# GpSimd waits for a batch's gathers to land before it issues the next batch's

## The chip, the cores and the metric

The kernel runs on one core of a Trainium2 chip. The core has TensorE (PE, matrix products), VectorE (DVE), ScalarE (ACT), GpSimd (POOL), SyncE (SP, which only issues transfers) and 16 DMA engines that all queues share. The metric is the device time of one execution in microseconds (us), lower is better.

## What is computed

Two layers, each of the form x + s * silu(g), on x of 8 batches of 512 tokens with 256 channels. The second layer, in whose last part the change lies:

```python
xn = _layernorm(x)
s = _hyena_fwd(xn, ...)      # projection, short convolution, long convolution by FFT, gate, projection
# g: a mixture of 20 experts, the 2 best of each token
top_vals, top_idx = jax.lax.top_k(probs, K)                     # K = 2
y = sum over e of gates[:, e] * (xf @ We[e] + be[e])            # gates: 0 but for the two chosen experts
x = x + s * _silu(y)
```

The first layer is causal attention with 16 heads (s) and a gated feed-forward network (g). All inputs and the output are float32.

## The kernel before

The kernel has three stages. Every engine runs its own program for each stage, and semaphores order them against each other.

**Attention stage.** It makes the first layer for each batch, normalises its result, picks two experts a token and scatters the token's row into `slots_in`, a table sorted by expert, with eight indirect transfers of 128 rows a batch (line 664, issued by GpSimd).

**Experts' stage.** 84 blocks of 128 rows are loaded from `slots_in`, multiplied with their expert's matrix (line 2032), get their expert's bias (line 2090) and go to `slots_out` (line 2062). It ends some 842 us into the span.

**Convolution stage.** It runs over the batches b = 0 to 7. A turn of TensorE is `pe_turn(b)`: the projection of batch b+1 (line 340), the first inverse product of b (line 373), the transposes of b+1 (line 362), the second inverse product of b (line 373), the forward transform of b+1 (line 317, four parts of 12 matmuls, each part with one increment of `vf_ps` at its end) and the output projection of b (line 408). ScalarE copies the projection out of PSUM (`projected`, line 419), does the first tap of the short filter (line 428), splits v into its high part (line 434), scales the rows of the first expert of a token (`first_choice`, line 2130), copies the four parts of the spectrum out of PSUM (`transformed`, line 442) and takes the silu (line 2136). VectorE multiplies the spectrum with the filter (`with_filter`, lines 481 to 524), does the other taps (line 457), the low part of v (line 464), the gate (line 551), adds the rows of the second expert (`second_choice`, line 2142), adds the output bias (line 558) and finishes the result (lines 2150 and 2154). Each engine takes these steps in the order written in `convolution_scalar`, `convolution_vector` and `pe_turn`.

GpSimd's only work in this stage is to gather the experts' rows of each token from `slots_out`: for batch n eight indirect transfers of 128 rows (two experts, four tiles of tokens) into `yg[:, n % 2]`, each adding 16 to `got[n % 2]`, so that a batch adds 128. `yg` has two buffers. Batch n's gathers may start when `acc_sb` is at n - 1, that is when VectorE has added the second expert's rows of batch n - 2 and the buffer is free. `acc_sb` at or below zero is not waited for, so batches 0 and 1 have no such wait. Ahead of each batch's gathers stands a one-column multiply into `idle_q` (line 2251), in a chain with itself over the semaphore `idle`. The users of the rows, `first_choice` and `second_choice`, wait for `got` themselves.

Of the kernel before, what the change touches and what calls it, by code (L numbers as in the profile page):

```python
# [47 lines left out]
def at_least(eng, sem, value):  # L48

    if isinstance(value, int) and value <= 0:  # L50
        return
    eng.wait_ge(sem, value)

def program(nc, x, wqkvT, woutT, wguT, wdT, wg1, bg1, wg2, bg2, winT, bin_, short, wo2, bo2, fw1, fb1, fw2, fb2,
# [15 lines left out]
    with ctx:  # L71
# [2042 lines left out]
        X = {n: sem("x_" + n) for n in "idle prem acc_sb sg_sb prod out_sb".split()}  # L2114
# [127 lines left out]
        def convolution_gpsimd(pool):  # L2242
            pool.wait_ge(W["kept"], NBLK)
            pool.memset(vt[:, :, 0:1], 0.0)
            pool.memset(vt[:, :, T + 1:T + 2], 0.0).then_inc(U["edges"], 1)
            for h_ in range(2):
                pool.wait_ge(yb_out[h_], 16 * NI)
            for n in range(B):
                at_least(pool, X["acc_sb"], n - 1)
                at_least(pool, X["idle"], n)  # L2250
                pool.tensor_tensor(idle_q[:, 3:4], ramp_col[:, :], ramp_col[:, :], ALU.mult
                                   ).then_inc(X["idle"], 1)
                for k in range(TOPK):
                    for t in range(NT):
                        pool.indirect_dma_start(yg[:, n % 2, k, t, :], None, slots_out,  # L2255
                                                bass.IndirectOffsetOnAxis(pos[:, n, t, k:k + 1], axis=0)
                                                ).then_inc(X["got"][n % 2], 16)

        with nc.Block() as block:
            @block.sync  # L2260
            def _(sp):
                attention_sync(sp)
                experts_sync(sp)
                convolution_sync(sp)

            @block.tensor
            def _(pe):
                attention_tensor(pe)
                experts_tensor(pe)
                convolution_tensor(pe)  # L2270

            @block.scalar
            def _(act):
                attention_scalar(act)
                experts_scalar(act)
                convolution_scalar(act)

            @block.vector
            def _(dve):
                attention_vector(dve)  # L2280
                experts_vector(dve)
                convolution_vector(dve)

            @block.gpsimd
            def _(pool):
                attention_gpsimd(pool)
                convolution_gpsimd(pool)
# [57 lines left out]
```

## Time and profile before

| | us |
|---|---|
| median of 3 runs | 1039.91 (1037.98 to 1041.28) |
| profiled execution | 1047.65 |
| its span, first to last instruction | 1045.9 |
| TensorE busy in the span | 954.6 (91%) |
| VectorE busy | 685.5 (66%) |
| ScalarE busy | 467.8 (45%) |
| GpSimd busy | 327.5 (31%) |

Times in rows are us from the span's start. A row of the timeline has the start, the duration, the engine, the source line, the operation, output and inputs, the form and the count of merged instructions; in brackets stands the engine's idle time before it and what ended it ("issue": nothing that the profile shows; "remote": a semaphore that moved long after the instruction that should have moved it). TensorE's rows show when a matmul is issued; its end is modelled, so that when its result was there is seen from those who wait for it. Shares of busy time are averages over the whole span; the change concerns its last 200 us alone.

### The profile page before, as it was taken

How to read it: one execution, taken by the hardware profiler on the slowest of the kernel's cores; microseconds unless marked ns; L12 is line 12 of the kernel's file. 1: busy time of each engine (PE TensorE's matmuls, PEld its weight loads, DVE VectorE, ACT ScalarE, POOL GpSimd, SP SyncE). 2: the span in 40 equal slices, each digit the busy share in tenths (PEclk: the TensorE clock that was granted, in tenths of full speed). 3: DMA queues.
4: the chain of work that ended last, by engine and by line, in shares of the span. 5: the costliest groups of instructions: out<-in, count | busy, mean ns of one | idle time of the engine just before them, and what ended most of it. 6: DMA issues, size and time to landing. Idle time of an engine off the chain costs nothing.

```text
span 1045.9 us, 18938 instructions
## 1 busy us (share of the span) xinstructions
PE 954.6 (91%) x5844; PEld 720.9 (69%) x5844; DVE 685.5 (66%) x1451; ACT 467.8 (45%) x871; POOL 327.5 (31%) x605
## 2 busy tenths in 40 slices
PE   8789999999999999999999999775889995999996
PEld 6666865866776775775776766464657783888885
DVE  6474676667577577577577466444566334899998
ACT  4346456446455555545546545442222332444442
POOL 5223224513612613613614522513000044322220
PEclk9899999979999999999999997986999996999999
DMA  7955856335535534644544620456876652443431
GB/s 268 117 152 88 184 139 88 110 131 79 113 141 83 122 141 71 124 151 63 102 161 63 134 82 2 142 157 197 250 235 209 193 181 67 125 156 123 132 106 44
DMA packets 88187, 136.70 MB, mean 131 GB/s; under 512 B 9987, under 2 KB 63939, under 8 KB 86084
## 3 DMA queue, kind: packets, MB, share of 16 engines
q1 hardware_dynamic: 69636, 100.75, 40.0%
q0 software_dynamic: 6144, 16.79, 5.3%
q10 hardware_dynamic: 12352, 18.48, 5.1%
q8 instruction: 28, 0.46, 0.2%
q14 instruction: 27, 0.22, 0.1%
HBM read 79.36 MB, written 55.57 MB: 129 GB/s over the span
## 4 chain that ended last, share of the span: by engine, by line
PE 32%; issue 31%; POOL 13%; DVE 11%; SPq 4%; ACT 2%; DMA 2%; another core or an unknown queue 1%; POOLq 0%; DVEq 0%; ACTq 0%
POOL PT L1850 6%; PE PS L2032 5%; PE PS L1053 3%; PE PS L373 3%; PE PS L1067 3%; PE PS L1025 3%; POOL slots_in L664 3%; PE PS L317 3%; DVE tmp L481 3%; POOL h L1833 3%; PE PS L828 3%; SPq L1968 2%; PE PS L340 2%; POOL idle_p L1844 2%; SPq L1972 1%
## 5 line engine op out<-in xcount | busy, mean ns | idle before, releaser
L1562 DVE TENSOR_REDUCE Mneg<-PS 128x2 f32<-128x1024 f32 (+2 forms) x192 | 195.0, 1043 | 70.3 <-PE PS L1029 69.3
L1316 ACT ACTIVATE PT<-PS 128x512 f32<-128x512 f32 (+1 forms) x384 | 172.7, 530 | 122.8 <-PE PS L1053 120.8
L1025 PE MATMUL PS<-ks,qs 96*128 96x256 f32 (+3 forms) x512 | 122.0, 348 | 3.1 <-issue 2.1
L1053 PE MATMUL PS<-qs,ks 96*128 96x512 f32 (+3 forms) x512 | 122.2, 358 | 2.6 <-ACT PT L1316 1.5
L1844 POOL TENSOR_TENSOR idle_p<-neghalf 128x1 f32<-128x1 f32 x128 | 25.2, 196 | 307.7 <-ACT PT L1316 307.7
L1053 PEld LDWEIGHTS PS<-qs,ks 96*128 96x128 f32 x512 | 89.1, 195 | 37.5 <-ACT PT L1316 18.4
L828 PE MATMUL PS<-xnT,Wgu 128*128 128x512 f32 x384 | 103.3, 410 | 8.5 <-DVE h L1505 8.4
L2032 PE MATMUL PS<-Wes,xbT 128*128 x336 | 98.6, 405 | 3.4 <-issue 2.5
L1850 POOL TENSOR_SCALAR_AFFINE_SELECT PT<-PT 128x256 f32<-128x256 f32 x256 | 98.9, 410 | 0.0
L1067 PE MATMUL PS<-PT,V 128*32 128x512 f32 (+3 forms) x1024 | 88.0, 451 | 5.9 <-POOL PT L1850 4.9
L828 PEld LDWEIGHTS PS<-xnT,Wgu 128*128 128x128 f32 x384 | 69.9, 191 | 31.4 <-DVE h L1505 11.8
L1025 PEld LDWEIGHTS PS<-ks,qs 96*128 96x128 f32 x512 | 77.7, 197 | 14.0 <-issue 10.0
L2090 DVE TENSOR_TENSOR yb<-PS,bes 128x256 f32<-128x256 f32 x84 | 35.3, 424 | 59.0 <-PE PS L2032 47.7
L2032 PEld LDWEIGHTS PS<-Wes,xbT 128*128 128x128 f32 x336 | 54.5, 197 | 22.6 <-issue 19.4
L1833 POOL TENSOR_TENSOR h<-h,h 128x512 fp32r<-128x512 f32 x40 | 51.3, 1290 | 59.4 <-ACT h L1280 59.2
L2054 ACT ACTIVATE xbT<-PS 128x256 f32<-128x256 f32 x84 | 31.5, 383 | 84.4 <-PE PS L2015 73.6
L664 POOL DMA_INDIRECT slots_in<-xn,rows_now x64 | 62.4, 975 | 17.5 <-issue 17.2
L2255 POOL DMA_INDIRECT yg<-slots_out,pos x64 | 61.5, 961 | 18.6 <-issue 17.6
L1505 DVE SCALAR_TENSOR_TENSOR h<-PS,sil 128x512 f32<-128x512 f32 x48 | 32.5, 689 | 49.4 <-ACT sil L1273 38.3
L1029 PE MATMUL PS<-mask,ident 128*128 128x128 f16 (+2 forms) x352 | 63.8, 257 | 0.0
L317 PE MATMUL PS<-v,Fwd 128*128 128x256 f32 x432 | 56.8, 291 | 6.0 <-issue 6.0
L373 PE MATMUL PS<-Inv,Z 128*128 128x256 f32 x256 | 58.5, 382 | 3.0 <-DVE Z L522 2.5
(239 smaller groups left out, 1604.3 us busy)
## 6 DMA issues: line engine op xcount, KB each, us to landing
qs<-qk_parts SPq DMA_DIRECT2D x96, 128.0 KB
ks<-qk_parts SPq DMA_DIRECT2D x96, 128.0 KB
slots_out<-yb ACTq DMA_DIRECT2D x28, 384.0 KB, 3.3
xb<-slots_in SPq DMA_DIRECT2D x83, 128.0 KB, 2.8
qk_parts<-qhl SPq DMA_DIRECT2D x16, 512.0 KB, 2.7
qk_parts<-khl SPq DMA_DIRECT2D x16, 512.0 KB, 3.1
xn2T_parts<-xn2T SPq DMA_DIRECT2D x8, 1024.0 KB, 4.9
xT<-xn2T_parts ACTq DMA_DIRECT2D x7, 1024.0 KB
```

The lines of the kernel that those rows point to most:

```text
L317: last = pe.matmul(PS[:, bank, C * (q_ % 2):C * (q_ % 2) + C], Fwd[:, i, kc, P * q_:P * q_ + P], src[:, j, 2 * half + kc, :], start=n == 0 ...
L373: last = pe.matmul(PS[:, 6 + m, C * z:C * z + C], Z[:, z, c, P * m:P * m + P], Inv[:, c, :], start=c == 0, stop=c == NQ - 1)
L664: pool.indirect_dma_start(slots_in, bass.IndirectOffsetOnAxis(rows_now[:, t, k:k + 1], axis=0), xn2[:, t, :], None).then_inc(S["sent"], 16)
L828: last = pe.matmul(out, lhs(i, c), rhs(j, c), start=last is None, stop=n == 0)
L1025: pe.matmul(out, qs[:, hd, P * qt:P * qt + P], ks[:, hd, 0:keys], start=n % a_bank == 0, stop=False, skip_group_check=True)
L1053: last = pe.matmul(PS[:, 4 + n, col:col + T - P * kt], ks[:, hd, P * kt:P * kt + P], qs[:, hd, P * kt:T], start=True, stop=True)
L1067: last = pe.matmul(PS[32 * j:32 * j + 32, 7, P * kt:T], V[:, kt, GH * g + j, :], PT[:, g % 2, j, COL[kt]:COL[kt] + T - P * kt], start=kt = ...
L1316: act.activation(PT[:, g % 2, j, 512 * n:512 * n + width], PS[:, 4 + n, 0:width], ACT.Exp, scale=SCALE).then_inc(S["exped"], 1)
L1562: dve.tensor_reduce(out=Mneg[:, 0, qt, heads[0]:heads[-1] + 1], in_=all_of, op=ALU.max, axis=AX.X, negate=True).then_inc(S["maxed"], 1)
L1833: pool.tensor_tensor(h[:, i, LO, :], h32[:, i % 2, :], f(h[:, i, HI, :]), ALU.subtract).then_inc(S["h_lo"], 1)
L1850: last = pool.affine_select(out=blocks, in_=blocks, compare_op=ALU.is_ge, fill=0.0, base=0, pattern=[[0, 2], [1, P]], channel_multiplier=-1)
L2032: ins = pe.matmul(PS[:, HALF + u % HALF, 0:C], xbT[:, u, c, :], Wes[:, bass.ds(expert, 1), c, :].rearrange("p o n -> p (o n)"), start=c == ...
```

## The change

After the wait for `acc_sb` and ahead of the multiply, GpSimd also waits, from batch 1 on, until `got` of the batch before is complete, that is until all eight of its gathers have landed.

```diff
             for n in range(B):
                 at_least(pool, X["acc_sb"], n - 1)
+                if n > 0:
+                    pool.wait_ge(X["got"][(n - 1) % 2], 128 * ((n - 1) // 2 + 1))
                 at_least(pool, X["idle"], n)
                 pool.tensor_tensor(idle_q[:, 3:4], ramp_col[:, :], ramp_col[:, :], ALU.mult
                                    ).then_inc(X["idle"], 1)
```

## Rows read from the trace of the kernel before

**Rows 1.** Timeline of VectorE: second expert's rows, filter products, split of v.

```profile
861.48 1.67 DVE L2142 SCALAR_TENSOR_TENSOR acc<-yg,gates,acc 128x256 f32<-128x256 f32 x4 [4.35 <-ACT acc L2130]
...
902.11 0.69 DVE L481 TENSOR_TENSOR tmp<-Vf,HA 128x512 f32<-128x512 f32 x1 [1.23 <-ACT Vf L442]
...
925.75 0.69 DVE L481 TENSOR_TENSOR tmp<-Vf,HA 128x512 f32<-128x512 f32 x1 [1.09 <-ACT Vf L442]
...
944.35 1.22 DVE L464 TENSOR_TENSOR v<-PS,v 128x1024 fp32r<-128x1024 f32 x1
...
949.43 0.69 DVE L481 TENSOR_TENSOR tmp<-Vf,HA 128x512 f32<-128x512 f32 x1 [1.09 <-ACT Vf L442]
```

**Rows 2.** Timeline of GpSimd: gathers and the multiply ahead of a batch.

```profile
847.73 1.32 POOL L2255 DMA_INDIRECT yg<-slots_out,pos  x1 [0.51 <-issue]
...
856.88 0.94 POOL L2255 DMA_INDIRECT yg<-slots_out,pos  x1 [0.30 <-issue]
...
858.19 0.98 POOL L2255 DMA_INDIRECT yg<-slots_out,pos  x1 [0.15 <-POOL idle_q L2251]
...
877.35 0.95 POOL L2255 DMA_INDIRECT yg<-slots_out,pos  x1 [0.30 <-issue]
900.96 0.19 POOL L2251 TENSOR_TENSOR idle_q<-ident 128x1 f32<-128x1 f32 x1 [22.67 <-DVE acc L2142]
...
957.54 0.95 POOL L2255 DMA_INDIRECT yg<-slots_out,pos  x1 [0.30 <-issue]
```

**Rows 3.** Timeline of TensorE: first turn, and a later one.

```profile
842.89 5.74 PE L340 MATMUL PS<-xT,Win 128*128 128x512 f32 x24 [0.69 <-DVE yb L2090]
...
856.05 5.74 PE L317 MATMUL PS<-v,Fwd 128*128 128x256 f32 x45
862.68 0.28 PE L317 MATMUL PS<-v,Fwd 128*128 128x256 f32 x1 [0.88 <-issue]
...
882.96 7.83 PE L340 MATMUL PS<-xT,Win 128*128 128x512 f32 x24
...
945.62 6.02 PE L317 MATMUL PS<-v,Fwd 128*128 128x256 f32 x48
...
954.74 5.83 PE L340 MATMUL PS<-xT,Win 128*128 128x512 f32 x24
```

**Rows 4.** Two windows: length, busy time of PE, PEld, DVE, ACT, POOL; clock, DMA share, GB/s.

```profile
862.00:867.00 5.00, 1.19 (x5) 0.79 (x5) 1.15 (x3) 0.00 (x0) 4.02 (x4) 0.99 0.38 105
867.00:872.00 5.00, 3.43 (x7) 1.57 (x6) 0.92 (x2) 0.60 (x1) 3.99 (x5) 0.50 0.35 102
```

**Rows 5.** Timeline of ScalarE: first expert's rows, spectrum copies, split of v.

```profile
859.74 1.71 ACT L2130 ACTIVATE acc<-yg,gates 128x256 f32<-128x256 f32 x4 [5.73 <-DMA yg<-slots_out,pos]
...
870.45 0.60 ACT L442 ACTIVATE Vf<-PS 128x512 f32<-128x512 f32 x1 [8.53 <-remote]
881.73 1.08 ACT L442 ACTIVATE Vf<-PS 128x512 f32<-128x512 f32 x2 [10.68 <-remote]
...
942.02 1.02 ACT L434 ACTIVATE v<-PS 128x1024 fp32r<-128x1024 f32 x1 [2.23 <-PE PS L362]
```

**Rows 6.** DMA queues from 862 to 882 (packets, MB, share): the answer's only queue.

```profile
q0 software_dynamic: 672, 1.84, 32.3%
```

**Rows 7.** Timeline of ScalarE: copies of the projection, first turn and a later one.

```profile
844.72 0.69 ACT L419 ACTIVATE vt<-PS,binc 128x512 f32<-128x512 f32 x1 [4.77 <-PE PS L340]
...
958.73 0.69 ACT L419 ACTIVATE vt<-PS,binc 128x512 f32<-128x512 f32 x1 [5.51 <-PE PS L340]
960.19 0.69 ACT L419 ACTIVATE vt<-PS,binc 128x512 f32<-128x512 f32 x1 [0.77 <-PE PS L340]
```

**Rows 8.** Timeline of all engines at the last burst of scatters.

```profile
719.93 0.57 PE L1238 MATMUL PS<-spread,ones 128*128 128x84 f32 x4
720.60 0.96 POOL L664 DMA_INDIRECT slots_in<-xn,rows_now  x1 [0.30 <-issue]
...
723.15 0.24 DVE L1780 TENSOR_SCALAR block_expert<-PS 128x84 int32<-128x84 f32 x1 [3.94 <-remote]
```

## The prediction

> **What bounds the kernel now.** I first asked what the changed line can touch: the stage in which all five engines run the convolution and mix the experts' rows, from 842 us of the span to its end. I read that stage engine by engine in the timeline. From the third turn on it is VectorE's: the first filter product of a batch starts at 925.75 and the next one's at 949.43 [rows 1], so a turn takes 23.68 us, and between these two VectorE sits idle for little but the 1.09 us ahead of each. GpSimd is far from that bound: the eight gathers of a batch, from 847.73 to 857.82 for batch 0, take 10 us [rows 2]. A later gather would therefore cost nothing in itself.
>
> The first turn does not look like that. The filter products of batch 1 could start when VectorE has added the second expert of batch 0, at 861.48 + 1.67 = 863.15; those of batch 2 start only at 902.11 [rows 1]. That is 38.96 us, where the later turns take 23.68. The missing 15.3 us lie in TensorE's rows: 45 of the 48 transform matmuls (line 317) of batch 1 go out at full pace, then single matmuls with 0.9 to 1.5 us between them, put down to "issue", until at 882.96 the next projection starts [rows 3]. From the transform's start to the next projection this turn takes 882.96 - 856.05 = 26.91 us, a later one 954.74 - 945.62 = 9.12 [rows 3]. In the same stretch the granted clock falls to 0.50, the lower level of 1.2 GHz, after TensorE has already been mostly idle for 5 us at 0.99 [rows 4], so the clock follows the stall and is not its start.
>
> ScalarE's rows tell what kind of stall it is. Its second spectrum copy starts at 870.45 after 8.53 us of idle time with the releaser "remote", the next at 881.73 after 10.68 us [rows 5]. Each waits only for matmuls that TensorE's own rows have as issued before 861.8 [rows 3]. So matmuls go in and their completions come out late, and in the end come all at once. Inside a part of the transform no matmul waits for a semaphore, and the only DMA queue with packets between 862 and 882 is GpSimd's, q0, at 32% of the engines [rows 6]: neither the experts' weights nor code are being loaded.
>
> What runs beside it is GpSimd. It issues 24 gathers without a break, 847.73 to 878.30 [rows 2]: batch 1 and batch 2 have both buffers and no acc_sb that is still missing. From batch 3 on it waits for acc_sb and issues eight at a time (for batch 3 until 900.96, after 22.67 us of idle time) [rows 2]. Two more places bear on whether a gather burst and late completions belong together. In a later turn ScalarE's first projection copy starts at 958.73, 3.99 us after the projection's first matmul, and the second at 960.19; the burst's last issue ends at 958.49 [rows 2, 3, 7]. With the first projection of the stage, before any gather runs, it is 844.72 - 842.89 = 1.83 us [rows 3, 7]. And at 719.93 four matmuls for the block table end a burst of scatters whose last issue ends at 721.56; VectorE gets their result only at 723.15, "remote" [rows 8]. So late in a burst of eight the completions are 2 to 3 us late, they come free 0.2 to 1.7 us after the burst, and after 24 in a row it takes until 881.73, 3.4 us. I read this as something that fills during a run of software gathers and empties when the run ends. What it is, the trace does not say.
>
> **The change, part by part.** It adds seven waits to GpSimd, one ahead of each batch from 1 on; it removes and moves nothing else. Behind the waiting instruction stand only the small multiply and this batch's eight gathers; the queues of SP and of ScalarE are not passed.
>
> Batches 3 to 7: the landing that is asked for is long past. Batch 3 asks for batch 2, issued by 878.30, at 900.96 [rows 2]; the later ones wait for acc_sb a turn further on in the same way. Cost 0, and the cover is the wait for acc_sb; without it a batch would start its gathers 1.9 us later, still ten microseconds or so before they are used.
>
> Batch 1: the last gather of batch 0 ends its issue at 857.82, and ScalarE gets the rows at 859.74 [rows 2, 5]. So the pause is 1.9 us and batch 1's gathers run from 860.1 to 870.1 instead of 858.19 to 868.2. Batch 2: one more such pause, 872.4 to 882.4, landed by 884.3. As data neither is missed: batch 1 is used 6.5 us ahead of VectorE's next filter product (in a later turn right behind the split of v, at 942.02 + 1.02 = 943.0 against 949.43 [rows 1, 5]), which is 880.4 even if that turn comes 15 us earlier, 8 us after the landing at 872.0.
>
> What the pauses do to the stall is the sum. If they empty what had filled, TensorE finishes the transform by 862 and the output projection by 865.2 (9.12 us after 856.05), ScalarE copies the spectra behind its mixing from 861.4 on, and VectorE starts batch 1 at 863.2 and batch 2 at 863.2 + 23.68 = 886.9 instead of 902.11: 15.2 us gained, with VectorE next in line. What is late next: the third burst now lies at 9 to 19 us of VectorE's turn, and its late part (from some 7 us into it, 879.5, to 1.7 us after it, 884.1) meets the transposes and the second inverse product, on which ScalarE's split of v at 942.02 - 925.75 = 16.3 us and VectorE's at 18.6 us of the turn wait [rows 1, 5]. Bounds: nothing, if VectorE's own work covers it; or VectorE's split, due at 881.8, waits for a release at 884.1 and ScalarE's 1.02 us: 3.3 us. I take the middle, 1.7, since the late completions of the later turns fall on cover and tell no more. Sum: -15.2 + 1.7 = -13.5 us, between -15.2 and -11.9. The profiled execution would go from 1047.65 us (span 1045.9 and 1.75 around it) to 1034.1, and the median of the runs from 1039.91 to 1026.4.
>
> The profiled execution is 7.74 us above that median, so the stall might not be in the plain runs. If it were in the profile alone, the plain runs should come, other things equal, to 1047.65 - 15.2 = 1032.4 or less; they are 7.5 us longer. That speaks for a stall in both.
>
> The Trainium skill, "Runtime: NRT & Kernel Launch", section "The ~15µs preamble/postamble breakdown", says that a profile's total is some 6.2 us above the reported execution time, whatever the kernel. By it 1047.65 would stand for 1041.4, which is close to the median and leaves the stall in the plain runs; no run here shows that figure by itself.
>
> **The rivals.** First, the stall belongs to the recording. For it: TensorE holds back matmuls that no semaphore is tied to, and VectorE and ScalarE, with few instructions, show no late completion of their own. Against it: the 7.5 us above. Then the plain runs have no such stall, the pauses cost and give nothing, and the time stays at 1039.9. 
> Second, slower: the pause is too short. If what fills needs longer than 1.9 us to empty, as the 3.4 us after 24 gathers could mean, it is not empty when batch 1's gathers begin, the stall goes on through batches 1 and 2 and ends as now 3.4 us after the last gather, which comes 3.8 to 4.1 us later: 1043.9. It decides at 1.9 us; the later bursts of eight come free in 0.2 to 1.7 [rows 2, 7], on the near side of it. 0.12.
>
> Third, the change does not reach the stall: it comes from something in the first turn other than the run's length, such as ScalarE's late start on the spectra behind the first gathers, at 859.74. The time stays at 1039.9. The late completions at other bursts speak against it. 0.06.
>
> **How the numbers follow.** The forecast, 1026.4, gets 0.57, since three bursts show the same lateness and the short ones come free by themselves. Its own range is 1023 to 1029: the bounds 1024.7 and 1028.0, and the runs' own spread of up to 1.9 us below and 1.4 above the median. The whole range goes on to 1041.5, to take in the two cases without an effect (0.31, at 1038.0 to 1041.3), and leaves out the slower one and the tails: about 0.2. A measurement of this kernel tells some 0.3% (3.1 us) from no change. Faster by more than that 0.57, within it 0.31, slower 0.12.
>
> **What would show it.** In the profile after: GpSimd idle for 1.9 us ahead of batches 1 and 2; no "remote" wait of the spectrum copies; transform and output projection of batch 1 done by 866; granted clock 1.00 from 862 to 890; VectorE's products of batch 2 at 887 to 890. If all of that is there and the plain time stays, the stall was the recording's. If single matmuls with a microsecond between them still stand from 862 to 885, the pause was too short or the reason is another; the forecast is wrong in both cases.

## The result and the profile after

| | before | after |
|---|---|---|
| median of the runs, us | 1040.60 (1037.98 to 1052.73, 4 runs) | 1063.34 (1061.53 to 1070.96, 4 runs) |
| profiled execution, us | 1047.65 | 1061.53 |
| its span, us | 1045.9 | 1059.8 |
| convolution stage in it: first projection matmul to the span's end, us | 1045.9 - 842.89 = 203.0 | 1059.8 - 833.71 = 226.1 |
| GpSimd busy, us | 327.5 | 418.5 |

The kernel became slower: 1.0219 times the time before, 95% interval 1.0181 to 1.0258, some 22.7 us. The forecast was 13.5 us faster, and the result lies above the whole range. Where the stage begins differs from execution to execution, with the same code in front of it (833 here, 843 before), so what follows compares the stage's own length: 23.1 us more, about what the medians say. Medians here and below are of all runs; the ratios leave out a run more than 1.5% above the fastest of its kernel, which of the changed kernels concerns one run, in the experiment of the cheap gap.

The stall that the prediction is about is gone. Timeline of TensorE after, first turn (columns as ahead of the rows of before):

```profile
846.92 6.10 PE L317 MATMUL PS<-v,Fwd 128*128 128x256 f32 x48
852.86 3.61 PE L408 MATMUL PS<-Wo,o 128*128 128x256 f32 x16
856.12 5.83 PE L340 MATMUL PS<-xT,Win 128*128 128x512 f32 x24
```

All 48 transform matmuls run as one group and the next projection starts 9.20 us after the transform's first matmul, against 26.91 before [rows 3] and 9.12 in the forecast. ScalarE, after, confirms it: its four spectrum copies run as one group, with no "remote" between them [rows 5].

```profile
850.58 1.71 ACT L2130 ACTIVATE acc<-yg,gates 128x256 f32<-128x256 f32 x4 [5.70 <-DMA yg<-slots_out,pos]
852.19 2.03 ACT L442 ACTIVATE Vf<-PS 128x512 f32<-128x512 f32 x4
```

What is new stands on GpSimd. Its timeline after: batch 1, the held gather of batch 2, the start of batch 3 and one gather of batch 7.

```profile
850.62 0.20 POOL L2253 TENSOR_TENSOR idle_q<-ident 128x1 f32<-128x1 f32 x1 [1.91 <-DMA yg<-slots_out,pos]
850.96 0.99 POOL L2257 DMA_INDIRECT yg<-slots_out,pos  x1
...
853.50 0.95 POOL L2257 DMA_INDIRECT yg<-slots_out,pos  x1 [0.30 <-issue]
854.75 9.09 POOL L2257 DMA_INDIRECT yg<-slots_out,pos  x1 [0.30 <-issue]
864.15 2.69 POOL L2257 DMA_INDIRECT yg<-slots_out,pos  x1 [0.30 <-issue]
867.15 1.02 POOL L2257 DMA_INDIRECT yg<-slots_out,pos  x1 [0.30 <-issue]
868.48 3.36 POOL L2257 DMA_INDIRECT yg<-slots_out,pos  x1 [0.30 <-issue]
872.14 0.95 POOL L2257 DMA_INDIRECT yg<-slots_out,pos  x1 [0.30 <-issue]
877.06 0.20 POOL L2253 TENSOR_TENSOR idle_q<-ident 128x1 f32<-128x1 f32 x1 [3.97 <-issue]
...
880.31 9.91 POOL L2257 DMA_INDIRECT yg<-slots_out,pos  x1 [0.31 <-issue]
...
905.80 0.19 POOL L2253 TENSOR_TENSOR idle_q<-ident 128x1 f32<-128x1 f32 x1 [5.07 <-issue]
...
1022.20 12.92 POOL L2257 DMA_INDIRECT yg<-slots_out,pos  x1 [0.31 <-issue]
```

The pause of 1.91 us is there as forecast. But from the fourth gather of batch 1 on, one gather in each burst takes 9.1 to 12.9 us to issue, and in batches 1 to 6 two more take 2.7 and 3.4, where those of before took 0.94 to 1.32 [rows 2]. The burst of batch 1 takes 872.14 + 0.95 - 850.96 = 22.1 us instead of 10, the later ones 22 to 23. Two lines of the view by source line say it for all 64 (durations in ns: smallest, median, largest); the first is after, the second before.

```profile
L2257 POOL DMA_INDIRECT yg<-slots_out,pos x64: 943/996/12922, 838.4 to 1040.4; - x64
```

```profile
L2255 POOL DMA_INDIRECT yg<-slots_out,pos x64: 940/946/1324, 847.7 to 1004.9; - x64
```

VectorE's timeline after tells when such a gather comes free:

```profile
853.91 0.69 DVE L481 TENSOR_TENSOR tmp<-Vf,HA 128x512 f32<-128x512 f32 x1
...
862.94 1.28 DVE L558 TENSOR_TENSOR s<-PS,bo2b 128x512 f32<-128x512 f32 x2
...
865.94 2.73 DVE L457 SCALAR_TENSOR_TENSOR cv<-vt,shortc,cv 128x512 f32<-128x512 f32 x4
...
869.79 1.22 DVE L2150 TENSOR_TENSOR acc<-sg,s 128x1024 f32<-128x1024 f32 x1
871.05 1.23 DVE L2154 TENSOR_TENSOR sg<-acc,x1b 128x1024 f32<-128x1024 f32 x1
...
878.70 1.67 DVE L2142 SCALAR_TENSOR_TENSOR acc<-yg,gates,acc 128x256 f32<-128x256 f32 x4 [2.81 <-ACT acc L2130]
880.29 0.68 DVE L481 TENSOR_TENSOR tmp<-Vf,HA 128x512 f32<-128x512 f32 x1
...
889.33 1.28 DVE L558 TENSOR_TENSOR s<-PS,bo2b 128x512 f32<-128x512 f32 x2
...
1022.18 0.68 DVE L481 TENSOR_TENSOR tmp<-Vf,HA 128x512 f32<-128x512 f32 x1
...
1034.22 0.68 DVE L558 TENSOR_TENSOR s<-PS,bo2b 128x512 f32<-128x512 f32 x1
```

Take 0.95 us, the undisturbed issue, off the end of a held gather: 854.75 + 9.09 - 0.95 = 862.89, 880.31 + 9.91 - 0.95 = 889.27, 1022.20 + 12.92 - 0.95 = 1034.17. Each time that is 0.05 to 0.06 us before VectorE starts line 558, the first instruction behind fifteen filter products (in the last turn twenty) that takes an input from PSUM. The 2.69 us gather gives 864.15 + 2.69 - 0.95 = 865.89, where line 457, a scalar_tensor_tensor, starts at 865.94. The 3.36 us gather gives 868.48 + 3.36 - 0.95 = 870.89. There no input comes from PSUM, but VectorE has a gap: line 2154 waits for line 2150 and starts 1.26 us behind it, where the next instruction of the same size, line 464 at 872.19, starts 1.14 us behind line 2154. So a gather, once it is held, stays held for as long as VectorE goes from one tensor_tensor with both inputs in SBUF straight to the next.

Not every such row holds a gather. In the kernel before, products follow each other 0.60 to 0.65 us apart, and the gathers beside them take 0.95 us; in the burst that begins at 948.75 all but the first start within 0.01 us of a product, as the gather of 957.54 [rows 2] does:

```profile
957.54 0.72 DVE L481 TENSOR_TENSOR tmp<-Vf,HN 128x512 f32<-128x512 f32 x1
```

From the first held gather on the engines run in lock step. The waits of the stage after (us in total, times, longest):

```profile
ACT acc L2130 <- DMA yg<-slots_out,pos: 68.9, 8, 19.7
...
DVE acc L2142 <- ACT acc L2130: 42.6, 8, 10.0
POOL idle_q L2253 <- issue: 27.5, 6, 5.1
```

Before, the first two were 5.7 and 4.3 us, once each, for batch 0, and GpSimd's third was a wait for `acc_sb`. Now ScalarE waits for rows in each turn, and behind that wait stand the four spectrum copies of the next batch. GpSimd's own wait ("issue" in the row) ends with the landing of the burst, within 0.1 us of ScalarE's start on its rows (876.96 and 877.06 for the rows of batch 1). It takes 4.0 to 5.1 us (for batch 2, 5.07 us; between 899 and 906 queue q1 moves 1.05 MB beside it), and only then do the next eight start. A turn is now GpSimd's: 905.80 - 877.06 = 28.74 us, of which 5.07 are the landing and 23.67 the burst. VectorE's first products of batches 2 and 7 are at 880.29 and 1022.18: 28.38 us a turn, where before it was 23.68 [rows 1]. The chain that ended last in after runs through the same gathers:

```profile
1014.48 4.47 issue
1018.95 0.20 POOL idle_q L2253
...
1022.20 12.92 POOL yg L2257
...
1040.44 2.72 DMA yg<-slots_out,pos
...
1043.18 0.03 ACT acc L2130
```

The account of the stage: up to the products of batch 2, 880.29 - 833.71 = 46.58 us against 902.11 - 842.89 = 59.22, so 12.64 gained; five turns of 4.70 us more, 23.5 lost; from the products of batch 7 to the end 37.6 against 1045.9 - 1020.49 = 25.4, 12.2 lost, since the last burst's rows arrive at 1043.18. Sum: +23.1 us.

### The profile page after: what moved, and what is told of

It is laid out like the page before. It is cut to its first block and busy times, and to the rows that moved or that the text cites. A ratio compares the mean times of both kernels' runs of the same rounds, so it can differ in the third digit from the quotient of the medians.

```text
span 1059.8 us, 18939 instructions
## 1 busy us (share of the span) xinstructions
PE 953.1 (90%) x5844; PEld 722.8 (68%) x5844; DVE 685.2 (65%) x1451; ACT 466.3 (44%) x871; POOL 418.5 (39%) x605
## 5 line engine op out<-in xcount | busy, mean ns | idle before, releaser
L2257 POOL DMA_INDIRECT yg<-slots_out,pos x64 | 151.5, 2367 | 21.2 <-issue 21.1
L1844 POOL TENSOR_TENSOR idle_p<-neghalf 128x1 f32<-128x1 f32 x128 | 25.4, 198 | 302.1 <-ACT PT L1316 302.1
L1025 PE MATMUL PS<-ks,qs 96*128 96x256 f32 (+3 forms) x512 | 118.8, 341 | 3.2 <-issue 2.1
L1053 PE MATMUL PS<-qs,ks 96*128 96x512 f32 (+3 forms) x512 | 118.4, 349 | 2.6 <-ACT PT L1316 1.5
L1053 PEld LDWEIGHTS PS<-qs,ks 96*128 96x128 f32 x512 | 85.6, 188 | 36.7 <-ACT PT L1316 19.1
L1025 PEld LDWEIGHTS PS<-ks,qs 96*128 96x128 f32 x512 | 75.5, 192 | 14.6 <-issue 8.9
L373 PE MATMUL PS<-Inv,Z 128*128 128x256 f32 x256 | 65.9, 416 | 5.8 <-DVE Z L522 4.1
L373 PEld LDWEIGHTS PS<-Inv,Z 128*128 128x128 f32 x256 | 53.6, 213 | 15.9 <-DVE Z L522 4.5
```

The lines of the kernel that those rows point to most:

```text
L373: last = pe.matmul(PS[:, 6 + m, C * z:C * z + C], Z[:, z, c, P * m:P * m + P], Inv[:, c, :], start=c == 0, stop=c == NQ - 1)
L1025: pe.matmul(out, qs[:, hd, P * qt:P * qt + P], ks[:, hd, 0:keys], start=n % a_bank == 0, stop=False, skip_group_check=True)
L1053: last = pe.matmul(PS[:, 4 + n, col:col + T - P * kt], ks[:, hd, P * kt:P * kt + P], qs[:, hd, P * kt:T], start=True, stop=True)
```

## The experiments

Each ratio below stands beside runs of the kernel before on the same chip; the chips differ (medians of before 1041 to 1050 us). Theory A: a gather is held while VectorE's filter products run without a gap, if the run itself began straight behind another instruction. In the kernel before each run of products starts out of 1.1 us of idle time [rows 1] and the gathers get in at instruction boundaries; in after, VectorE goes from the second expert's addition straight into the products, because that addition is what comes last. The loss then comes from the held gathers together with the lock step. Theory B: the form of the new wait makes the gathers slow. Theory C: a burst that begins inside a run of products is shut out, wherever the run started from.

**A wait ahead of the products (after plus one line).**

```diff
                 if b > 0:
+                    dve.wait_ge(X["sg_sb"], b)
                     for part in range(FILTER_PARTS - 2):
```

> The changed kernel with one more wait: VectorE waits for ScalarE's silu of the batch before (sg_sb) ahead of the filter products of batches 1 to 7, so that the run of filter products starts after 1 to 2 us of idle time instead of right behind the second expert's rows. Theory A (a run that starts behind another VectorE instruction shuts the gathers out; one that starts out of idle time lets them in): the gathers of batches 1 to 7 go back to 0.95 us each, a burst to 10 us, a turn from 28.4 to 24 to 26 us, and the time to 1030 to 1045. Theory B (the separate wait instruction of GpSimd does it) and theory C (what decides is that the burst reaches into a run that has begun): the third gather of a burst still takes some 9 to 10 us, and the time stays at 1061 to 1075.

1070.81 us, 1.0158 times before (1.0083 to 1.0233). The gathers are back at about 0.95 (mean 1.02 us over all 64, from 2.37), and GpSimd waits for `acc_sb` again, but the wait has a price of its own. Waits of the stage:

```profile
POOL idle_q L2254 <- DVE acc L2142: 80.9, 5, 19.4
...
DVE tmp L481 <- ACT sg L2136: 30.3, 6, 5.1
```

The silu is finished 5.05 us after VectorE would have begun, in each of six turns. A turn takes 28.95 us (batches 2 to 7), not the 24 to 26 expected. So the part of theory A on the gathers holds; the expected time failed, since the silu comes so much later than the edit assumed. A cheaper gap is needed (below).

**The form of the wait (before plus one line).**

```diff
                 at_least(pool, X["acc_sb"], n - 1)
+                if n > 1:
+                    pool.wait_ge(X["got"][n % 2], 128 * ((n - 2) // 2 + 1))
```

> The kernel before with a wait of the same form at the same place, but for the landing of batch n - 2, which is long past when GpSimd comes to it (from batch 2 on). Theory B (form of the wait): a gather of 9 us in each burst, and 1055 us or more. Theories A and C: gathers of 0.95 us, single matmuls a microsecond apart in the first turn as before, 1036 to 1050 us, no change from the kernel before.

1049.60 us against 1050.10, 0.9992 (0.9961 to 1.0022). The wait asks for the landing of the batch before last, which is long past.

```profile
L2257 POOL DMA_INDIRECT yg<-slots_out,pos x64: 942/948/1167, 840.1 to 1002.2; - x64
```

No gather is above 1.17 us. Here the wait never blocks; in the experiment ahead the change's own waits stand and the gathers are quick as well. So theory B falls.

**The third burst and all later ones held into the products (before plus one line).** `dstep` counts VectorE's filter products; the line makes GpSimd wait for the third of a turn, for batches 2 to 7.

```diff
                 at_least(pool, X["acc_sb"], n - 1)
+                if n > 1:
+                    pool.wait_ge(U["dstep"], ND * (n - 1) + 3)
```

> The kernel before, with GpSimd's gathers of batches 2 to 7 held until VectorE has done three filter products of the batch in hand (dstep), some 2 us into the run that starts out of idle time; no landing is waited for. Theory A (start out of idle time decides): gathers of 0.95 us, 1036 to 1050 us. Theory C (a burst that starts inside a run is shut out): gathers of 7 us and more in batches 2 to 7, bursts of some 20 us as in the changed kernel; the time then 1030 to 1055, since two buffers still cover a burst of 23 us.

1036.24 us, 0.9840 (0.9784 to 0.9897). GpSimd and ScalarE in the first turn:

```profile
869.63 0.52 POOL L2253 TENSOR_TENSOR idle_q<-ident 128x1 f32<-128x1 f32 x1 [5.27 <-issue]
870.29 1.26 POOL L2257 DMA_INDIRECT yg<-slots_out,pos  x1
871.86 1.46 POOL L2257 DMA_INDIRECT yg<-slots_out,pos  x1 [0.31 <-issue]
```

```profile
866.96 1.58 ACT L442 ACTIVATE Vf<-PS 128x512 f32<-128x512 f32 x3 [7.25 <-remote]
```

The burst begins inside the run that started at 867.59 out of 8.28 us of idle time, and its gathers wait for the next boundary, 1.26 and 1.46 us, and no more; in all six such bursts none is above 1.46: theory C falls. And the run of 24 gathers, cut to 16 and 8 by a pause of 5.27 us, leaves one "remote" wait of 7.25 us, over 27.9 us into the stage, where before there are two, the last over at 881.73 - 842.89 = 38.8 [rows 5]. The stage takes 196.2 us.

**No idle time ahead of the products (before plus extra work).** Two additions, whose result nothing reads, fill the gap; GpSimd's program is that of before.

```diff
                 if b > 0:
+                    for half in range(2):
+                        wo = Wo2[:, :, :].rearrange("p a c -> p (a c)")
+                        dve.scalar_tensor_tensor(out=xn2[...], in0=wo, scalar=gate(0, 0, 0), in1=wo, ...)
                     for part in range(FILTER_PARTS - 2):
```

> The kernel before, with two more VectorE instructions of some 0.66 us (scalar_tensor_tensor on constants, into a dead tile) ahead of the filter products of each batch, so that the run starts without the 1.1 us of idle time; GpSimd's program is untouched. They are extra work and feed nothing. Theory A (start out of idle time decides): from batch 3 on a gather of 7 to 10 us in each burst, as in the changed kernel, without any wait for a landing; the time 1040 to 1060. Theories B and C: gathers stay at 0.95 us, and the time at 1038 to 1046 (7 x 0.2 us more work).

1052.34 us, 1.0020 (0.9982 to 1.0058). Two of the five bursts from batch 3 on are held as in after, three are not; the first gathers of batches 3 and 5:

```profile
905.63 10.35 POOL L2259 DMA_INDIRECT yg<-slots_out,pos  x1
...
955.87 1.32 POOL L2259 DMA_INDIRECT yg<-slots_out,pos  x1
```

Both start 0.4 us ahead of a run of products that has no idle time in front of it (906.02 and 956.25). The other two that are let in (batches 4 and 7) differ from these in that GpSimd's multiply ahead of the burst is still running as the products begin. Theory A expected a hold in each of the five: the missing gap makes a hold possible and does not decide it alone. It also shows what two buffers are worth: the held burst takes 23.5 us, and the time does not change, since its rows are wanted a whole turn later.

**A cheap gap (after plus one line).** VectorE waits for its own last addition.

```diff
                 if b > 0:
+                    dve.wait_ge(X["acc_sb"], b)
                     for part in range(FILTER_PARTS - 2):
```

> The changed kernel with a wait of VectorE for its own sum of the batch before (acc_sb) ahead of the filter products of batches 1 to 7: the run then starts some 0.1 us later, out of a short idle time, and nothing else is held up. Theory A1 (any idle time ahead of the run lets the gathers in): gathers of 0.95 to 1.5 us, bursts of 10 to 11 us, a turn of 24 us, no stretch of single matmuls in the first turn, and the time 10 to 20 us below the kernel before of the same chip. Theory A2 (it takes the microsecond and more that the kernel before has there, or the gathers' place decides): a gather of 9 us in each burst as in the changed kernel, and the time 10 to 25 us above the kernel before.

1038.56 us, 0.9873 (0.9805 to 0.9942), with the change in it. The fourth gather of batch 1, 9.09 us in after, and the products of batch 1:

```profile
878.72 1.39 POOL L2258 DMA_INDIRECT yg<-slots_out,pos  x1 [0.30 <-issue]
```

```profile
876.29 1.68 DVE L2142 SCALAR_TENSOR_TENSOR acc<-yg,gates,acc 128x256 f32<-128x256 f32 x4 [4.17 <-ACT acc L2130]
878.00 0.69 DVE L481 TENSOR_TENSOR tmp<-Vf,HA 128x512 f32<-128x512 f32 x1
```

The products start 1.71 us behind the second expert's addition, where in after it is 853.91 - 852.32 = 1.59. So the wait costs 0.12 us here, and that is enough: theory A1 holds and A2 falls. In the later turns the products start out of 1.14 to 1.28 us of idle time, about as in the kernel before [rows 1]. Bursts take 9.7 to 12.2 us (longest gather 3.36), TensorE's first turn has no single matmuls, and the stage takes 193.1 us in an execution that is the longest of its four (1051.95 us, with the stage beginning only at 857.1). A tenth of a microsecond of VectorE a turn turns +2.2% into -1.3%.

**The lock step lifted (after, waits for n = 1 and 2 alone).**

```diff
-                if n > 0:
+                if 0 < n < 3:
                     pool.wait_ge(X["got"][(n - 1) % 2], 128 * ((n - 1) // 2 + 1))
```

> The changed kernel without the waits of batches 3 to 7, so that GpSimd waits for a landing ahead of batches 1 and 2 alone. If a burst that is shut out costs time only because the next one has to wait for its landing (lock-step), GpSimd gets a batch ahead again by batch 4 or 5, ScalarE waits for rows in two or three turns instead of seven, and the time is 1 to 12 us below the kernel before. If the shut-out itself is what costs, ScalarE waits for rows in every turn and the time stays 8 us and more above the kernel before.

1043.62 us, 0.9950 (0.9912 to 0.9989). Bursts 1 and 2 are held just as in after (9.10 and 9.91 us); the third follows the second at once and takes 10.2 us; it meets a run of products that begins without a gap (911.04) and is not held, its longest gather taking 1.42. VectorE's products of batches 2, 3, 4 and 5 start at 882.76, 911.04, 940.25 and 964.46: two turns of 28 to 29 us, then 24.2, the products out of idle time again from batch 4 on; GpSimd waits for `acc_sb` again from batch 5 on, as the first expectation had it. The two stages are 203.6 and, in after, 226.1 us; the two ratios, each beside its own runs of before, are 2.7% apart. So the waits from batch 3 on, costed at nothing in the prediction, keep the loss alive: each held burst makes the next run of products start without a gap, and the next burst lies beside it.

**One pause alone (before plus the hold of batch 2).**

```diff
                 at_least(pool, X["acc_sb"], n - 1)
+                if n == 2:
+                    pool.wait_ge(U["dstep"], ND * (n - 1) + 3)
```

> The kernel before with one pause alone: GpSimd's gathers of batch 2 are held until VectorE has done three filter products of batch 1 (dstep). Batches 0 and 1 go out as one run of 16, batches 3 to 7 as before. If the pause in the first run of gathers was what made the kernel with all six such waits faster by 14 us, this one is faster by 10 to 16 us too, with a stretch of late matmuls of 5 to 9 us in place of 20. If the six later waits made it, 0 to 3 us.

1042.62 us, 0.9941 (0.9906 to 0.9975), 6 us gained and less than expected. The first turn is like that of the third experiment; the later turns are 24.2 us here and 23.5 there, which over five turns is 3.5 us. Kernels whose later bursts are not held differ among themselves, though: 23.7 us a turn in the kernel before and in the control below, 24.1 in the kernel of the second experiment, on the chip of the third. So the holds of the later bursts look worth 0.2 to 0.7 us a turn, and no run here gives that with an interval. In this trace VectorE waits some 0.4 us in each later turn for ScalarE's first tap, which itself follows a projection whose completion comes late in the burst, as in [rows 7]; with the bursts held into the products that wait is not there; in the kernel before it is there in one later turn only.

**Everything together (before plus three waits).**

```diff
                 if b > 0:
+                    dve.wait_ge(X["acc_sb"], b)
                     for part in range(FILTER_PARTS - 2):
 ...
                 at_least(pool, X["acc_sb"], n - 1)
+                if n == 1:
+                    pool.wait_ge(X["got"][0], 128)
+                if n > 1:
+                    pool.wait_ge(U["dstep"], ND * (n - 1) + 3)
```

> The three helpful parts together: GpSimd waits for the landing of batch 0 ahead of batch 1, holds batches 2 to 7 until VectorE has done three filter products of the batch in hand, and VectorE waits for its own sum ahead of each run of products. If the parts add (first turn without late matmuls as in the kernel with the short idle time, later turns of 23.5 us as in the kernel with all six holds): the stage from the first projection to the end takes 186 to 192 us where the kernel before takes 203 to 209, and the time is 13 to 20 us below the kernel before. If the holds bring the shut-out back, gathers of 7 us and more, and a gain of less than 8 us.

1028.92 us, 0.9861 (0.9808 to 0.9913), shorter than both kernels. The stage takes 188.6 us; turns are 23.5 us, gathers at most 1.47 us but for one of 3.36, and the first turn has no single matmuls. The gain of 15.6 us lies in the range that was expected if the parts add; but the third experiment has 0.9840 with the holds alone, so that the times do not show that they add. Only the stages, one execution each, differ (188.6 and 196.2 us).

**A gap inside the run (after plus one line).** In the middle of the products VectorE waits for its own product 9, the one just ahead.

```diff
             if part == 3:
+                if b > 0:
+                    done(9)
                 mul(q[3], im(0), tb(HN, 1))
```

> The changed kernel with one wait of VectorE on its own last product after nine products of a run (dstep), so that a run of 15 instructions on SBUF has a pause of some 0.1 us in its middle, and none at its start. If a pause in the run is what lets a shut-out gather in, the third gather of each burst ends there: 6 to 7 us instead of 9.9, and those behind it take 0.95 to 1.5 us until the run ends; the time falls by 10 us or more below the changed kernel. If it takes a pause at the start of the run, or an instruction that reads PSUM, 9.9 us as in the changed kernel.

A single execution took 1033.54 us, beside 1044.56 before; then with an interval:

> The kernel after with one wait of VectorE for its own products inside each run of products, at the start of part 3, now with an interval. If the loss of the change comes from the shut-out gathers alone, and the stall of the first turn is out of the plain runs as it is out of the profile, the time is 0.985 to 0.993 of before, as the version with the pause ahead of the run gave (0.987, 0.980 to 0.994). If the one look at 0.989 was a lucky run, it is at 1.00 to 1.02, with gathers of 9 us again.

1028.48 us, 0.9858 (0.9797 to 0.9919). GpSimd and VectorE in the first turn:

```profile
853.46 5.49 POOL L2259 DMA_INDIRECT yg<-slots_out,pos  x1 [0.30 <-issue]
859.25 1.02 POOL L2259 DMA_INDIRECT yg<-slots_out,pos  x1 [0.30 <-issue]
860.58 0.95 POOL L2259 DMA_INDIRECT yg<-slots_out,pos  x1 [0.30 <-issue]
```

```profile
856.85 1.28 DVE L481 TENSOR_TENSOR tmq<-Vf,HB 128x512 f32<-128x512 f32 x2
858.16 0.69 DVE L481 TENSOR_TENSOR tmq<-Vf,HN 128x512 f32<-128x512 f32 x1
```

Products of the run start 0.60 us apart, so line 481 would have gone on at 858.05; it starts at 858.16. At that gap of 0.11 us the held gather gets in: 853.46 + 5.49 - 0.95 = 858.00, again 0.05 us ahead of the boundary. Those behind it in the burst issue in 0.95 to 1.44 us although the products go on without a gap; the longest of all later ones takes 3.36, and from batch 4 on GpSimd is ahead again and waits for `acc_sb`. The stage takes 190.6 us, and 204.6 in the control below, on the same chip. This is the plainest evidence that the loss comes from the held gathers: with the waits of the change untouched, a tenth of a microsecond per turn on VectorE takes it away.

**The control (before plus VectorE's own wait).**

> The kernel before with nothing but VectorE's wait for its own last addition ahead of a batch's products; GpSimd's program is as before, so the run of 24 gathers in the first turn is whole. It is the control for the two versions that have this wait and pauses between the bursts (0.987 and 0.986 of the time before). If their gain comes from the pauses of GpSimd, this kernel keeps the single matmuls with a microsecond between them in the first turn and takes the time of before, 0.995 to 1.005 of it. If the gain comes from the wait itself (VectorE's products or TensorE's completions fare better for it), it is at 0.985 to 0.99 and the single matmuls are gone or fewer. The pitch of the later turns, 23.7 us before, tells the same: 23.5 or less only in the second case.

1040.61 us against 1041.47, 0.9995 (0.9961 to 1.0030). TensorE and ScalarE in the first turn:

```profile
865.25 0.58 PE L408 MATMUL PS<-Wo,o 128*128 128x256 f32 x1 [1.54 <-issue]
868.03 0.58 PE L408 MATMUL PS<-Wo,o 128*128 128x256 f32 x1 [2.20 <-issue]
```

```profile
863.85 0.60 ACT L442 ACTIVATE Vf<-PS 128x512 f32<-128x512 f32 x1 [11.30 <-remote]
```

The single matmuls and the "remote" waits are all there, and the products of batch 2 start 891.09 - 832.08 = 59.0 us into the stage, as before (59.2). The wait alone gives nothing; what the two versions with it and with pauses gain (0.9873 and 0.9861) takes the pauses of GpSimd.

## Why the prediction was wrong, step by step

**The stall and its price: right.** Runs of gathers without a pause bring TensorE's completions late, and the pause of 1.91 us ends that: transform to projection 9.20 us, no "remote" copies, the products of batch 1 straight behind the second expert's addition, all as forecast. The price agrees as well, within wide intervals. Where the gathers are let in, the change gives 0.9873 and 0.9858, that is -13.3 and -14.8 us of the time before beside them (intervals -6.1 to -20.5 and -8.4 to -21.1), beside the -13.5 of the sum; by the stages on one chip the second gains 14.0 (190.6 against 204.6 in the control). Both have a line of VectorE's more than the change, which the control shows to be worth nothing by itself in the first of them. In after itself, 12.64 us were gained up to the products of batch 2, of the 15.2 forecast.

**The step that failed** is the sentence "As data neither is missed", with the times behind it, batch 1's gathers "from 860.1 to 870.1". The 10 us of a burst were read from batch 0's, which ends before any filter product of this stage starts, and they hold in the later turns of before, where the products start out of 1.09 us of idle time [rows 1, 2]. They were moved into a turn that, by the forecast's own numbers (863.15 and 863.2), has no such idle time. There the burst takes 22 to 23 us. The rows showed gathers beside products at 0.95 us and I took that for a constant. That a gather can be held for 9 us could not be read from the trace of before, where no gather takes above 1.32 us; that the two situations differ could.

**"Batches 3 to 7 ... Cost 0" failed with it.** The cover named there, the wait for `acc_sb`, is there only as long as a burst takes 10 us. With 23 us it is gone, the landing becomes the last condition, and the new wait ties the next burst to the end of this one. The second pause, put at 1.9 us like the first, was a longer one as well, 3.97 us; where the burst ahead of it is let in (the cheap gap) it is 1.92. The sixth experiment gives the size of the failure: 22.5 us of the stage between the kernel with and without these waits, in one execution each. Neither failure makes the loss alone: in the sixth experiment two bursts are held as in after and the kernel is still 0.5% faster than before, and with the waits kept but a gap on VectorE it is 1.4% faster.

**The third burst's +1.7 us** for meeting the transposes cannot be seen in after, where that burst is held; in the versions that let it in, the sums come out within their intervals with or without it.

**The clock** was forecast at 1.00 from 862 to 890. The two windows after (columns as in [rows 4]):

```profile
862.00:867.00 5.00, 3.41 (x16) 2.66 (x14) 5.00 (x9) 0.68 (x1) 4.54 (x2) 1.00 0.67 236
867.00:872.00 5.00, 3.23 (x13) 2.57 (x14) 4.97 (x7) 1.02 (x1) 4.38 (x2) 0.76 0.18 52
```

It stays at 1.00 in the first and still falls to 0.76 in the second, where TensorE has waited 3.32 us for VectorE's short filter; before it was 0.50 there. The stage began 9.18 us earlier in this execution; moved by that, the forecast's range is 852.8 to 880.8, and of its windows of 5 us only 867.8 to 872.8 (0.68) and the next (0.98) are below 1.00. Before, the clock was at 0.50 from 867 to 887. So the forecast missed this dip, which comes behind another wait than the stall.

**The rivals.** That the stall belongs to the recording (0.25) falls: kernels that lose it in the profile and hold no burst for long (the cheap gap, everything together, the gap inside the run) are 1.3 to 1.4% shorter in plain runs, and the control that keeps it is not. The 7.74 us between profile and median in before were no constant of the recording: in after the profiled execution, 1061.53 us, is the shortest of the four runs. That the pause is too short (0.12, the slower side) did not happen: the stall is gone. The kernel is slower by a mechanism that was not on the list. The third, that the change does not reach the stall, falls as well.

## What to carry to other kernels

A duration read beside one state of the neighbour engine holds for that state; when a change removes idle time, ask what used to slip through it. A wait on the landing of the batch before turns two buffers into one as soon as a burst grows, so bound it by the slowest burst, not by the usual one. And where GpSimd issues gathers beside a long row of VectorE work, a gap of a tenth of a microsecond in the row may be worth more than the time that it costs.

## What the runs showed of the hardware

VectorE's tensor_tensor instructions with both inputs in SBUF, 0.69 us each, held one GpSimd gather over 20 of them in a row (12.92 us); the first instruction that reads PSUM, a scalar_tensor_tensor, or a gap of 0.11 us let it in. Rows that began out of 1.1 us of idle time or more let gathers in between their first fifteen products in 1.47 us at most. The other way round a gather costs VectorE little: a product that meets one is some 0.04 us longer (0.73 instead of 0.69).

The Trainium skill, "SBUF — State Buffer", section "Who interferes with whom", says that a VectorE instruction with two SBUF inputs contends with a GpSimd instruction that reads SBUF, and that tensor_tensor was not seen to stall a DMA, since it takes only the shared read interface and descriptor generation needs the write interface, which it calls inferred. The Trainium skill, "SBUF — State Buffer", section "SBUF: two separate sides", says that whoever starts first has the shared ports for the whole instruction. Contention between such instructions is what these traces show, but the hold spans up to 20 instructions and does reach the issue of a gather, and a scalar_tensor_tensor with two SBUF inputs (lines 457 and 2142) let gathers through in 1.0 us. Here the measurement decides.

Open: why a row lets gathers in or not; of the bursts that met a row without a gap ahead of it, three of five in the fourth experiment and the third burst of the sixth were let in, one of them with the same start, to 0.01 us, as a held one; and what it is that fills on TensorE's side during a long run of gathers. The runs show that a pause of 1.9 us after eight empties it; with 16 in a row (the third experiment) the products of batch 2 start 53.3 us into the stage, with 24 in a row (before) 59.2, with eight (after) 46.6.
